# Operand loads at set tiles of the preceding head, projection two matmuls to a slot, rows by halves

## The reference, cut to what matters

```python
x = x + attention_block(groupnorm(x))        # x: 2 x 16 x 128 x 1024, fp32; 32 groups of 32 channels
# tokens n = 2048 per batch element, 8 heads looking back, 8 looking ahead, head size 64
q, k, v = (einsum('bnd,hed->bhne', xf, W) for W in (Wq, Wk, Wv))
p = softmax(mask(q @ k.T / 8))               # i >= j for the first 8 heads, i <= j for the others
o = concat heads of (p @ v), shape B, 16 heads, n, 64
out = o.reshape(B, n, D) @ Wo.T              # 128 output rows come from one head alone
```

## Time and profile before

| | |
|---|---|
| median of 3 runs | 3388.7 us (3385.54 to 3389.45) |
| the profiled execution | 3384.05 us, its span 3382.3 us |
| TensorE (PE) busy | 3139.5 us, 93% |
| VectorE (DVE) busy | 1980.5 us, 59% |
| GpSimd (POOL) busy | 1265.1 us, 37% |
| mean granted TensorE clock | 0.973 |
| a head, from its slot 0 to the next | 64.9 us |
| the same with a loop return in it | 72.0 to 73.4 us |

### The profile page before, as it was taken

The page is one execution under the profiler, slowest core; times in us unless marked ns, Lnnn a source line. Parts: engine busy times, 40 slices in busy tenths (PEclk is TensorE's granted clock), DMA queues, the critical chain, the costliest instruction groups (busy, mean ns, idle before and its releaser), DMA issues.

```text
span 3382.3 us, 48803 instructions
## 1 busy us (share of the span) xinstructions
PE 3139.5 (93%) x14472; PEld 2518.3 (74%) x14472; DVE 1980.5 (59%) x3540; ACT 1582.9 (47%) x3173; POOL 1265.1 (37%) x996
## 2 busy tenths in 40 slices
PE   4999799799999789999999999999999899989998
PEld 3788688588888557777777777777777777777776
DVE  6212211411121288777777778788787777877785
ACT  2210111311111066666656666666666666665665
POOL 2000000200000145556545555566565555655564
PEclk9999899899999889999999999999999999999999
DMA  6546534543443635333433243335233423343330
GB/s 236 150 131 148 155 119 99 178 145 106 117 139 100 128 91 116 66 75 76 91 70 75 63 98 76 70 70 111 63 75 81 94 62 75 72 90 75 71 66 19
DMA packets 345293, 333.55 MB, mean 99 GB/s; under 512 B 275456, under 2 KB 275456, under 8 KB 332800
## 3 DMA queue, kind: packets, MB, share of 16 engines
q1 hardware_dynamic: 345088, 331.40, 40.3%
HBM read 213.91 MB, written 117.44 MB: 98 GB/s over the span
## 4 chain that ended last, share of the span: by engine, by line
PE 51%; DVE 9%; issue 5%; DMA 0%; ACT 0%; DVEq 0%; SPq 0%; ACTq 0%
PE rows L1020 11%; PE max L955 7%; PE acc L1002 6%; PE scores L988 6%; PE acc L1006 6%; PE acc L1004 6%; PE scores L983 6%; DVE part_max L876 3%; DVE o_full L924 2%; DVE p_low L684 2%; PE side L965 1%; PE scores L986 1%; DVE inv L903 1%; DVE inv L910 1%; DVE max L870 0%
## 5 line engine op out<-in xcount | busy, mean ns | idle before, releaser
L684 POOL TENSOR_TENSOR p_low<-probs,p_high 128x512 fp32r<-128x512 f32 (+2 forms) x960 | 1208.7, 1276 | 975.3 <-ACT p_high L809 968.2
L805 ACT ACTIVATE probs<-scores 128x512 f32<-128x512 f32 (+3 forms) x1280 | 686.6, 536 | 749.8 <-PE scores L988 642.9
L876 DVE TENSOR_REDUCE part_max<-max 128x1 f32<-128x512 f32 (+3 forms) x1280 | 766.0, 603 | 205.6 <-PE max L955 184.4
L809 ACT ACTIVATE p_high<-scores 128x512 fp32r<-128x512 f32 (+3 forms) x1280 | 682.7, 533 | 0.0
L955 PE MATMUL max<-k,q 128*128 128x512 f32 (+3 forms) x1280 | 490.1, 384 | 124.1 <-DVE part_max L876 106.1
L326 DVE TENSOR_TENSOR stage_l<-proj,stage_h 128x512 fp32r<-128x512 f32 x192 | 132.2, 690 | 683.2 <-ACT stage_h L318 659.3
L988 PE MATMUL scores<-q,k 128*128 128x512 f32 (+3 forms) x1280 | 493.6, 386 | 0.0
L318 ACT ACTIVATE stage_h<-proj 128x512 fp32r<-128x512 f32 x192 | 114.7, 599 | 804.2 <-PE proj L264 424.6
L1002 PE MATMUL acc<-p_high,v 128*128 128x512 f32 (+3 forms) x1280 | 474.0, 370 | 9.6 <-DVE p_low L684 9.6
L983 PE MATMUL scores<-q,k 128*128 128x512 f32 (+3 forms) x1280 | 477.6, 373 | 0.3 <-ACT p_high L809 0.3
L1006 PE MATMUL acc<-p_low,v 128*128 128x512 f32 (+3 forms) x1280 | 471.3, 368 | 0.0
(11 more groups left out here) (86 smaller groups left out, 4332.3 us busy)
## 6 DMA issues: line engine op xcount, KB each, us to landing
xs<-xT SPq DMA_DIRECT2D x64, 512.0 KB, 4.9
qk_h<-stage_h SPq DMA_DIRECT2D x128, 256.0 KB, 2.6
qk_l<-stage_l SPq DMA_DIRECT2D x128, 256.0 KB, 3.0
q<-qk_h SPq DMA_DIRECT2D x64, 512.0 KB, 8.0
k<-qk_h SPq DMA_DIRECT2D x64, 512.0 KB, 11.1
w_raw<-wqk SPq DMA_DIRECT2D x32, 512.0 KB, 4.1
v_h<-stage_h SPq DMA_DIRECT2D x64, 256.0 KB, 2.6
v_l<-stage_l SPq DMA_DIRECT2D x64, 256.0 KB, 3.1
```

The source lines that it names most:

```text
L684: eng.tensor_tensor(p_low[:, n % 4, part], probs[:, n % 4, part], p_high[:, n % 4, part].bitcast(F32), ALU.subtract).then_inc(done, 1)
L805: nc.scalar.activation(probs[:, n % 4, 0:cols], scores[n % 2][:, 0:cols], ACT.Exp, scale=SCALE).then_inc(exp_done, 1)
L809: nc.scalar.activation(p_high[:, n % 4, 0:cols], scores[n % 2][:, 0:cols], ACT.Exp, scale=SCALE).then_inc(high_act, 1)
L876: nc.vector.tensor_reduce(part_max[:, s % 2, at, m:m + 1], max_bank[n % 2][:, 0:cols], AX.X, ALU.max).then_inc(max_read, 1)
```

## The change

The projection is cut into 24 pieces of 2 matmuls, in slots 9 to 20 (first half of the columns) and 23 to 34 (second half); the adds move to slots 21 and 35. SyncE issues the loads for the next head while the current one runs, each held back by a wait on `weighed`, the count of value tiles done: q1 and the first k1 when 2 tiles of the current head are done, their other halves at 5, q2 and k2 at 8, the high part of v at 11, the low part at 15. Only the loads for the first two heads are issued as before. The residual rows are loaded, added and stored by halves of 512 columns, each half with semaphores of its own.

```diff
-OP_PIECES = 6
+OP_PIECES = 24
-OP_SLOT = {0: 9, 1: 10, 2: 11, 3: 15, 4: 16, 5: 17}
-ADD_SLOT = {0: 13, 1: 19}
+OP_SLOT = {n: (9, 23)[n // 12] + n % 12 for n in range(OP_PIECES)}
+ADD_SLOT = {0: 21, 1: 35}
+LOAD_TILE = (2, 5, 8, 11, 15)
...
-                reached(sp, scored, count(i, p, S_TILES, -S_TILES))
-                for dst, loaded, kept, key in (
...
+                def at(tile):
+                    if during is not None:
+                        sp.wait_ge(weighed, count(*during, S_TILES, tile))
+
+                for dst, loaded, kept, key, tile in (
+                        (q1[0:E], first_loaded, qk_h, False, LOAD_TILE[0]), (k1[0:E], first_loaded, qk_h, True, None),
+                        (q1[E:P], first_loaded, qk_h, False, LOAD_TILE[1]), (k1[E:P], first_loaded, qk_l, True, None),
+                        (q2[0:E], second_loaded, qk_l, False, LOAD_TILE[2]), (k2[0:E], second_loaded, qk_h, True, None)):
+                    if tile is not None:
+                        at(tile)
...
-                reached(sp, weighed, count(i, p, S_TILES, -S_TILES))
-                for cols, kept in ((slice(0, E), v_h), (slice(2 * E, 3 * E), v_l)):
+                for cols, kept, tile in ((slice(0, E), v_h, LOAD_TILE[3]), (slice(2 * E, 3 * E), v_l, LOAD_TILE[4])):
+                    at(tile)
...
+            def residual(g, half):
+                reached(sp, stored[half], g * 16)
+                sp.dma_start(res[:, half, :], x_res[bass.ds(g, 1)].rearrange("a p d -> (a p) d")
+                             [:, half * NQ:(half + 1) * NQ]).then_inc(res_loaded[half], 16)
+
+            def rows_out(g, half):
+                sp.wait_ge(added, g * 2 + (half + 1))
+                sp.dma_start(out[bass.ds(g, 1)].rearrange("a p d -> (a p) d")[:, half * NQ:(half + 1) * NQ],
+                             res[:, half, :]).then_inc(stored[half], 16)
...
-                        load_head(*((i, 1) if p == 0 else (i + 1, 0)), of)
+                        load_head(*((i, 1) if p == 0 else (i + 1, 0)), of,
+                                  None if first_head(i, p) else (i, p))
...
-                        rows_out(before)
-                        residual(before + 1)
+                        for half in range(2):
+                            rows_out(before, half)
+                            residual(before + 1, half)
...
-                    half, third = n // 3, n % 3
+                    half, piece = n // 12, n % 12
...
-                    for k in range(third * 8, third * 8 + 8):
+                    for k in range(piece * 2, piece * 2 + 2):
...
-                    if third == 2:
+                    if piece == 11:
                         last.then_inc(projected, 1)
```

More of the change, by code:

```diff
@@ L585, in attend @@
         wo_split = sem("wo_split")
-        res_loaded = sem("res_loaded")
+        res_loaded = [sem(f"res_loaded{n}") for n in range(2)]
         cleared = sem("cleared")
@@ L610, in attend @@
         added = sem("added")
-        stored = sem("stored")
+        stored = [sem(f"rows_stored{n}") for n in range(2)]
         def pairs(eng, body):
@@ L646, in heads @@
             for half in range(2):
-                for n in range(3 * half, 3 * half + 3):
+                for n in range(12 * half, 12 * half + 12):
                     do("project", None, PAIRS, 0, n)
@@ L703, in _, with load_head @@
         def _(sp):
-            def load_head(i, p, kind):
+            def load_head(i, p, kind, during=None):
                 row = i + kind * PAIRS // 2
-                reached(sp, scored, count(i, p, S_TILES, -S_TILES))
-                for dst, loaded, kept, key in (
-                        (q1[0:E], first_loaded, qk_h, False), (k1[0:E], first_loaded, qk_h, True),
-                        (q1[E:P], first_loaded, qk_h, False), (k1[E:P], first_loaded, qk_l, True),
-                        (q2[0:E], second_loaded, qk_l, False), (k2[0:E], second_loaded, qk_h, True)):
+                def at(tile):
[7 more added lines that the diff above has]
+                        at(tile)
@@ L745, in pair @@
                         sp.wait_ge(wo_split, WO_UNITS)
-                        residual(0)
+                        for half in range(2):
+                            residual(0, half)
                     if p == 1 or not isinstance(i, int) or i > 0:
                         before = 2 * i + (p - 1)
-                        rows_out(before)
-                        residual(before + 1)
+                        for half in range(2):
+                            rows_out(before, half)
+                            residual(before + 1, half)
             pairs(sp, pair)
-            rows_out(G_HEADS - 1)
-            sp.wait_ge(stored, 16 * G_HEADS)
+            for half in range(2):
+                rows_out(G_HEADS - 1, half)
+            for half in range(2):
+                sp.wait_ge(stored[half], 16 * G_HEADS)
         @block.gpsimd
@@ L935, in do @@
                     dve.wait_ge(projected, count(i, p, 2, half - 1))
-                    dve.wait_ge(res_loaded, 16 * count(i, p, 1, 0))
+                    dve.wait_ge(res_loaded[half], 16 * count(i, p, 1, 0))
                     nc.vector.tensor_tensor(res[:, half, :], rows_bank[:, :], res[:, half, :],
@@ L1008, in do @@
                 elif step == "project":
-                    half, third = n // 3, n % 3
+                    half, piece = n // 12, n % 12
                     if n == 0:
                         pe.wait_ge(o_low_ready, count(i, p, 2, 0))
-                    if third == 0:
+                    if piece == 0:
                         reached(pe, added, count(i, p, 2, half - 2))
```

## The result

The changed kernel takes 3291.7 us (median of 4 runs, 3290.6 to 3292.7) against 3389.0 us (4 runs beside them, 3385.5 to 3389.5): a ratio of 0.9715, with a 95% interval of 0.9698 to 0.9732. The forecast was 3322 us, its range 3298 to 3363.

The account below looks back on a forecast made before the run. TensorE, busy 93% of the span, was taken as the bound, plus its waits for DVE. Returns 40 + projection 30 - DVE's blocks 3 = 67 us saved, so 3388.7 - 67 = 3322 us, range 3298 to 3363.

Parts of the forecast that it names:

- the size of the pause: At each of ten loop returns, DVE's pause was to fall from 8.12 to 4.1 us, with bounds 0 and 8.12.
- the 40: Saving forecast at the ten loop returns from the shorter pause: 81.3 - 10 x 4.1 = 40 us.
- a term put at nothing: In the head with a return, the granted clock averaging 0.95 costs nothing more, since TensorE waits for DVE anyway.
- the whole pause is paid: At a return, the 8.0 us between the two heads is one pause, falling in slots where DVE is the bound.
- The 3 us put down for DVE's blocks: In slots 9 to 20, POOL holding up DVE operations costs 0.1 us a head, 3 us in all.
- Slots 24 to 32: Projection work moved to slots 23 to 34 lets DVE's lag be made good: 1.0 us a head, 30 us.
- Interleaving: Projection in 12 visits of 2 matmuls for each half instead of 3 of 8: a visit costs nothing.
- the slower rival: Each projection visit exposes its weight load, fully 95 us, giving 3417; decides from 0.12 us a visit; chance 0.04.
- POOL in DVE's way: Slots 9 to 20: all eight DVE operations held up, 2.2 us lost a head, 3385; half, 3349; chance 0.15.
- the compressed slots would be the new bound: In slots 9 to 20, blocks as long as a POOL operation would make eight cost more than 3.9 us.
- The pause stays: At the returns, the 8 us are the fetch's own latency; only the projection gives, 3362; chance 0.15.
- The five waits and the rows by halves: In SyncE's queue, five load waits cost nothing; 64 half-size loads and stores replace 32 each, effect set to 0.

Follow-up runs that it names:

- the late add: Changed kernel with the projection's last four pieces in the next head's slots 1 to 4, their add in slot 9: 3310.6 us; add in slot 6: 3272.3 us.

## Why the prediction went wrong

**The steps that failed.** The first and largest is the size of the pause: "I take one such landing and half a microsecond of the tail of the new residual load: 4.1 us." It is 2.5 us. A landing of 512 KB was taken for the nearest row of a fetch, and nothing bore that out: with nothing ahead of it the pause is 2.3 to 2.5 us, and the residual, issued 2.0 us before, adds 0.16 us and not 0.5. So 81.3 - 25.2 = 56.1 us fell away, 16 more than the 40. By itself this would have given 3306 us, inside the range, which took in a pause of near 2 us. It took more to leave it.

The second step is a term put at nothing: "that the granted clock averages 0.95 in that head costs nothing more, since TensorE would wait for DVE anyway". The heads with a return gave 62.5 us, 6 more than their pauses. Before, TensorE stood still for 6.83 us, and its granted clock then fell to 0.50, the 1.2 GHz level, where matmuls of 512 columns start 0.43 us apart and not 0.23:

```profile
2026.00:2028.00 2.00, 0.85 (x2) 0.75 (x3) 1.86 (x5) 1.59 (x5) 0.00 (x0) 0.50 0.98 205
...
2027.75 0.63 PE L983 MATMUL scores<-q,k 128*128 128x512 f32 x1
2028.17 0.63 PE L988 MATMUL scores<-q,k 128*128 128x512 f32 x1
```

After, TensorE stands for 1.23 us and the clock is 1.00 in the whole head. From the first max unit behind the pause to that of slot 9 it took 11.1 to 11.6 us at the ten returns before and takes 10.6 to 10.7 after, 7.6 us less in all. That is about the size of the 6 us, but no run changed the clock alone. It also means that "the whole pause is paid" was right by luck: now some 0.7 us of each pause aren't paid (2.5 against 1.8), and before, the low clock cost about as much again.

**The rest of the difference.** The 3 us put down for DVE's blocks weren't paid, and the median lies 1.1 us over the profiled execution where it had been 4.6. Together: 16 + 6 + 3 + 3.5 = 29 of the 30 us missed; the range, drawn around a pause, had no room for the other three.

**Slots 24 to 32: right.** 1.0 us a head was forecast and 1.01 measured. TensorE's timeline through slots 30 and 31, answering to the earlier trace rows; no start is more than 0.29 us behind its forerunner:

```profile
2097.66 0.40 PE L1001 MATMUL scores<-q,k 128*128 128x512 f32 x1
2097.89 0.40 PE L1033 MATMUL rows<-wo_h,o_low 128*128 128x512 f32 x1
...
2099.11 0.45 PE L996 MATMUL scores<-q,k 128*128 128x512 f32 x1
2099.40 0.39 PE L1001 MATMUL scores<-q,k 128*128 128x512 f32 x1
```

**Interleaving: right.** Going from one sum into another costs 0.23 us, like any start, here 24 times a head; the slower rival with its 0.12 us a visit has nothing in the trace.

**POOL in DVE's way: it happened and cost nothing.** DVE's two pairs of divisions in slots 9 to 20 of the plain head, and POOL beside the first:

```profile
2065.99 2.54 DVE L937 TENSOR_TENSOR o_full<-acc_s,inv 64x256 f32<-64x256 f32 x2
...
2074.92 1.25 DVE L937 TENSOR_TENSOR o_full<-acc_s,inv 64x256 f32<-64x256 f32 x2
```

```profile
2066.66 1.41 POOL L686 TENSOR_TENSOR p_low<-probs,p_high 128x512 fp32r<-128x512 f32 x1 [0.22 <-ACT p_high L822]
```

The pair of divisions that meets POOL takes 2.54 us, the one that doesn't 1.25: 1.3 more, in one place. The others of the eight have their short form (the low parts 0.28, 0.68 and 0.68 us, the diagonal 0.69), so two at most were held up; outside these slots the diagonal at 2084.74 was too, with 1.62 us. TensorE is busy for 21.25 of 21.25 us there: the two units that DVE may be behind took it up, as the text had it. The trace agrees in kind with the rule of the Trainium skill ("SBUF — State Buffer", section "SBUF: two separate sides"); what was worked out beside it, that the compressed slots would be the new bound, did not come.

**The pause stays: wrong as a rival, right in part.** Ten pauses remain, and 2.4 us of each don't hang on any load. That agrees with the Trainium skill ("Runtime: NRT & Kernel Launch", section "Instruction fetch mechanics"): a taken branch whose target isn't at hand still costs a fetch. That the pause is this fetch is argued, from its place at the branch and from two engines that pause there and wait for nothing; no view shows the fetch itself. One argument for the rival was a misreading: at the return with 6.96 us not half of the loads were missing from the queue, for five of the six of q and k were issued ahead of the pause, the last of them at 2545.01.

**The five waits and the rows by halves** cost nothing, as forecast; but the residual's place is worth something that I hadn't seen: its last 256 KB stand 2.0 us clear of the pause. One slot later the pause is 1 us longer.

## What to carry to other kernels

Keep large transfers out of the last few microseconds before a loop's branch; behind the branch they may come all at once, and spreading them out further bought nothing here. When a bound engine alternates with slots in which another is the bound, move the divisible work of the first into the slots of the second, and look where its consumer then stands in the queue: the late add cost 1.8 us in one place and 0.7 in another. A stop of one engine can cost more than its length, if another's clock falls by it: look at the granted clock behind the stop before that term is put at nothing. And a range drawn around the largest term needs room for the small ones, which here all fell the same way.

## What the runs showed of the hardware

- The pause at a taken branch, for DVE in this loop: 2.3 to 2.5 us with nothing queued, 3.4 to 3.6 with a load of 256 KB issued 0.8 us ahead, 3.6 to 4.1 with two loads of 512 KB issued in the last 1.1 us, 8.1 to 8.5 with six loads of 512 KB ahead, the first of them 3.8 us. Loads issued after its start leave it at 2.3 to 2.9 us.
- DVE and ScalarE pause each for itself, ScalarE from 0.3 us later on: 3.6 and 5.4 us at the same return, and the head pays for the longer.
- Behind TensorE's stop of 6.83 us the granted clock was 0.50; behind one of 1.23 us it stayed at 1.00.
- How much a transfer adds, as a function of its size and lead, stays open, and with it why ScalarE's pause is the longer with loads in the queue: it begins 0.3 us later, so the same loads stand further ahead of it, and some that are behind DVE's start are ahead of its own.
